# Fourth expert stage of a four-layer sequence model: down product in three rounded products, three chunks behind the gate

## The reference

```python
inh = sigmoid(x @ Wr / temperature)
w = routing weights from inh (zone, or the two nearest experts)
y = sum_e w[..., e] * ((silu(x @ Wg[e]) * (x @ Wu[e])) @ Wd[e])
out = x_residual + y
```

## Time and profile before

| | us |
|---|---|
| median of three runs | 1958.83 |
| lowest and highest | 1954.51, 1964.04 |
| the profiled execution | 1963.8 |
| its span, first to last instruction | 1961.8 |
| TensorE busy | 1723.9 |
| DVE busy | 1198.0 |
| ACT busy | 974.3 |
| POOL busy | 847.5 |

### The profile page before, as it was taken

The page is one execution under the profiler, slowest core; times in us unless marked ns, Lnnn a source line. Parts: engine busy times, 40 slices in busy tenths (PEclk is TensorE's granted clock), DMA queues, the critical chain, the costliest instruction groups (busy, mean ns, idle before and its releaser), DMA issues.

```text
span 1961.8 us, 25458 instructions
## 1 busy us (share of the span) xinstructions
PE 1723.9 (88%) x8004; PEld 1314.2 (67%) x8004; DVE 1198.0 (61%) x2815; ACT 974.3 (50%) x1864; POOL 847.5 (43%) x852
## 2 busy tenths in 40 slices
PE   6989998659999998989999988888899888888799
PEld 6979997537767676767777655666665555555565
DVE  5552215658677767777776835544446666677765
ACT  3612002346556665665656567676545444445442
POOL 3842101225545454554555454443447666651100
PEclk9989558769999999999999989898999888889999
DMA  5001000168433333233324462231000101112233
GB/s 84 1 2 24 1 1 1 38 146 201 111 92 102 87 98 92 90 99 86 96 90 118 114 161 73 58 88 47 17 23 23 33 23 26 23 28 75 81 106 94
DMA packets 131182, 134.92 MB, mean 69 GB/s; under 512 B 56614, under 2 KB 75306, under 8 KB 131050
## 3 DMA queue, kind: packets, MB, share of 16 engines
q1 hardware_dynamic: 120904, 132.35, 25.3%
q10 hardware_dynamic: 10146, 0.94, 0.6%
HBM read 127.93 MB, written 5.31 MB: 68 GB/s over the span
## 4 chain that ended last, share of the span: by engine, by line
PE 36%; DVE 17%; ACT 11%; issue 7%; POOL 4%; DMA 2%; SPq 1%; DVEq 0%; ACTq 0%; POOLq 0%
PE ypsum L1122 7%; PE flow_G L100 4%; PE flow_G L102 3%; PE flow_G L101 3%; DVE flow_a L1666 2%; DVE flow_a L1672 2%; DVE flow_phi L1450 2%; DMA flow_raw<-in_L_ffn_expert_down_k 2%; POOL flow_alo L1753 2%; PE flow_U L100 2%; PE flow_U L101 2%; PE flow_U L102 1%; ACT flow_ahi L1152 1%; ACT xn_tokens L1184 1%; PE flow_side L100 1%
## 5 line engine op out<-in xcount | busy, mean ns | idle before, releaser
L1753 POOL TENSOR_TENSOR flow_alo<-flow_a,flow_ahi 128x512 fp32r<-128x512 f32 x264 | 342.0, 1295 | 345.6 <-ACT flow_ahi L1152 345.1
L100 PE MATMUL flow_G<-xn_hi,flow_hi 128*128 128x512 f32 x520 | 285.6, 549 | 49.5 <-DVE flow_a L1666 23.2
L1666 DVE TENSOR_TENSOR flow_a<-flow_G,flow_mask 128x512 f32<-128x512 f32 x256 | 175.7, 686 | 161.2 <-ACT flow_G L1326 137.9
L1326 ACT ACTIVATE flow_G<-flow_G 128x512 f32<-128x512 f32 x256 | 149.0, 582 | 140.2 <-PE flow_G L102 139.7
L101 PE MATMUL flow_G<-xn_lo,flow_hi 128*128 128x512 f32 x520 | 213.0, 410 | 0.0
L102 PE MATMUL flow_G<-xn_hi,flow_lo 128*128 128x512 f32 x520 | 211.7, 407 | 0.0
L1672 DVE TENSOR_TENSOR flow_a<-flow_U,flow_a 128x512 f32<-128x512 f32 x296 | 204.7, 691 | 9.9
L1152 ACT ACTIVATE flow_ahi<-flow_a 128x512 fp32r<-128x512 f32 x264 | 165.4, 627 | 85.3 <-DVE flow_a L1672 84.1
L1762 POOL TENSOR_TENSOR flow_b<-flow_b,flow_mask 128x512 f32<-128x512 f32 x96 | 127.1, 1329 | 147.3 <-ACT flow_b L1330 76.7
L100 PEld LDWEIGHTS flow_G<-xn_hi,flow_hi 128*128 128x128 f32 x520 | 102.7, 197 | 117.6 <-issue 44.6
L1762 POOL TENSOR_TENSOR flow_a<-flow_a,flow_mask 128x512 f32<-128x512 f32 x96 | 127.8, 1343 | 106.3 <-ACT flow_a L1330 54.7
(11 more groups left out here) (536 smaller groups left out, 3930.1 us busy)
## 6 DMA issues: line engine op xcount, KB each, us to landing
flow_mask<-mask_rows_top SPq DMA_DIRECT2D x512, 128.0 KB, 3.1
flow_mask<-mask_rows_top SPq DMA_DIRECT2D x64, 256.0 KB, 3.3
flow_mask<-mask_rows_zone SPq DMA_DIRECT2D x64, 256.0 KB, 3.2
flow_mask<-mask_rows_steps SPq DMA_DIRECT2D x32, 256.0 KB, 4.0
x<-in_L_attn_x SPq DMA_DIRECT2D x8, 256.0 KB, 5.5
flow_raw<-in_L_ffn_expert_gate_k SPq DMA_DIRECT2D x16, 128.0 KB, 3.6
flow_raw<-in_L_ffn_expert_up_k SPq DMA_DIRECT2D x16, 128.0 KB, 3.6
flow_raw<-in_L_ffn_expert_down_k SPq DMA_DIRECT2D x16, 128.0 KB, 4.1
```

The lines of the kernel that those rows point to most:

```text
L100: pe.matmul(out, w_hi, x_hi, start=start, stop=False)
L1326: act.activation(gate, gate, ACT.Silu).then_inc(ev["r_done"], 1)
L1666: dve.tensor_tensor(out, G[at % 2].psum[:, :], weight, ALU.mult).then_inc(ev["t_done"], 1)
L1753: pool.tensor_tensor(alo[i][:, :], acts[i][:, :], ahi[i][:, :].bitcast(F32), ALU.subtract)\
```

## The change

The fourth stage goes over to the first stage's way. Its down matrix is split too (three matrices in place of two), ACT rounds each chunk's activations, POOL makes the low part, TensorE does three rounded products in place of one f32 product, and it does them three chunks behind the gate in place of five. SiLU writes one of the four activation tiles; it waits for the down product four chunks back. The copy waits for the stage's own count of DVE products. The step "y" of the fourth stage comes two chunks earlier (0.9 in place of 3), and that of the other three stages 0.1 earlier (2.9 in place of 3), which puts it one iteration of ACT's loop earlier, ahead of that iteration's SiLU.

```diff
+        self.split = index in (0, 3)
...
-MOE_STEPS = joined(post_steps(3), {"act": ((3, "y"),), "sp": ((5.5, "store"),)})
+MOE_STEPS = [joined(post_steps(3), {"act": ((0.9 if l == 3 else 2.9, "y"),), "sp": ((5.5, "store"),)}) for l in range(4)]
...
+        def parts_no(at):
+            return at if at < first else at - hosts[3].first + first
+
         def wait_slot(eng, at):
 
+            if plan.chunk[at][0].split and at >= hosts[3].first + A_RING:
+                eng.wait_ge(ev["down_done"], at - A_RING + 1)
+                return
             eng.wait_ge(ev["down_done"], at - B_RING + 1 if at >= first + B_RING else first - A_RING + at % A_RING + 1)
 
         def b_tile(at):
+            if plan.chunk[at][0].split:
+                return acts[at % A_RING]
             return B[(at - first) % B_RING]
...
-                    if h.direct:
+                    if h.split:
+                        pe.wait_ge(ev["ahi_done"], parts_no(at) + 1)
+                        pe.wait_ge(ev["alo_done"], parts_no(at) + 1)
+                    else:
                         wait_filled(pe, at)
-                    else:
-                        pe.wait_ge(ev["ahi_done"], at + 1)
-                        pe.wait_ge(ev["alo_done"], at + 1)
...
-                    if h.direct:
+                    if not h.split:
...
-                downs = [(at + (DIRECT_LAG if h.direct else DOWN_LAG), at) for at, (h, _, _) in enumerate(plan.chunk)]
+                downs = [(at + (DOWN_LAG if h.split else DIRECT_LAG), at) for at, (h, _, _) in enumerate(plan.chunk)]
...
-                    n = len(moe.sources) - 1
+                    n = len(moe.sources) - (not hosts[h].split)
...
-                    act.wait_ge(ev["a_done"], at + 1)
+                    act.wait_ge(ev["a_done"], plan.up[at])
...
-                    if at and at - 1 < first:
+                    if 0 < at <= plan.end and plan.chunk[at - 1][0].split:
                         rounded(at - 1)
...
-                    pool.wait_ge(ev["ahi_done"], at + 1)
+                    pool.wait_ge(ev["ahi_done"], parts_no(at) + 1)
...
-                    if at and at - 1 < first:
+                    if 0 < at <= plan.end and plan.chunk[at - 1][0].split:
                         rest(at - 1)
```

More of the change, by code:

```diff
@@ L655, in steps @@
             for g in range(GROUPS):
-                out += [(self.place("moe", l, g, off), name, "moe", l, g) for off, name in MOE_STEPS[engine]
+                out += [(self.place("moe", l, g, off), name, "moe", l, g) for off, name in MOE_STEPS[l][engine]
                         if l < 3 or name in LAST_STEPS]
```

## The result

The changed kernel takes 1979.88 us (median of four runs, 1972.88 to 1982.99), the kernel before 1959.19 us in the four runs beside it: ratio 1.010, 95% interval 1.0069 to 1.0131. It is about 20 us slower, outside the range and on the side of rival (b). The profiled execution took 1982.99 us with a span of 1981.0 us and a granted clock of 0.911 (before 1963.8, 1961.8 and 0.916).

A forecast was written before the change was run, and what follows sets the result against it. TensorE was taken as the bound in three fourth-stage stretches, with DVE or ACT leading elsewhere. Terms -5.6 - 0.9 - 1.6 + 5.6 + 1.5 = -1.0 us gave a median of 1957.8 us, range 1947 to 1968.

The forecast's parts named there:

- rival (b): Fourth stage's 27 DVE-bound chunks: every mask product meets POOL's low part, 13 us lost, 1969.3 us; chance 0.12.
- ACT's copies: Fourth stage, where ACT loads tables: copies waiting for DVE delay the affinities queued behind; 5.6 us lost, bounds 1.9 and 8.
- the meeting: DVE-bound stretches of the fourth stage: POOL's low part overlaps DVE once in each of three, 1.5 us lost, bounds 0 and 13.
- the form's gain: Fourth stage's TensorE-bound stretches: three rounded products in place of one f32 save 0.15 us on 37 chunks, 5.6 us gained.
- The price of a chunk: TensorE-bound stretches of the fourth stage: a chunk takes 2.10 us in place of 2.25, saving 0.15.
- the tail's term: End of the fourth stage: lag three in place of five, y about 3.5 us after the last up multiplication starts, 0.9 gained.
- decision point: DVE-bound chunks: POOL makes DVE the bound once more than half of those mask products are over 1 us.
- those 27 chunks: Fourth stage's chunks in 1764:1803, 1827:1859 and 1889:1903, where DVE is the bound; 0.48 to 0.5 us lost each.
- the stage's start: Chunk 4 of the fourth stage: two more down products, 1.4 us of TensorE, costed within the copies' term.
- The order of y: y ahead of one SiLU delays it at group ends: taken as nothing, bounds 0 and 0.3 for each of 32 groups, 10.
- the sum's -1.6: First stage: the first down product's wait for y, 1.6 us in all, goes and is gained.
- Splits: Fourth stage's eight splits, done in the second stage, grow from two to three matrices: nothing, at most 2 us.

The follow-up runs named there:

- with y at 1: Changed kernel with the fourth stage's y at 1 in place of 0.9, one ACT iteration later: 1977.3 us, ratio 1.0060 to 1.0112, stage 214.7 us.
- the mask product from PSUM: Changed kernel with the fourth stage's SiLU left in its bank, so DVE's mask product reads PSUM and one SBUF tile: 1976.9 us, stage 212.2 us.
- the copy's other 3 us: Changed kernel with POOL copying the activations in place of subtracting: 1971.4 us; stage 6.0 us longer than with the fill, 2.8 seen in DVE's durations.
- a fill: Changed kernel with POOL filling the low part's tile with zeros in place of subtracting: 1966.4 us, ratio 1.0021 to 1.0057, stage 204.2 us.

## Why the prediction was wrong, point by point

The account of the stage: 197.3 before; -1.0 for the form itself without its helpers; +7.9 for ACT's copies; +11.0 for POOL's low part; 215.1. Split at the last gate product, the part ahead of it has +1.8, +7.5 and +9.6, the end -2.8, +0.4 and +1.4. Beside the forecast, two terms carry most of the miss of 22 us: the meeting (1.5 forecast, 9.6) and the form's gain (-5.6 forecast, +1.8).

- **The price of a chunk: right.** 2.10 to 2.11 us wherever TensorE led, and taking one more product away gave 8.0 us where the count of 37 chunks said 8.5. The method, distances between starts in a stretch that TensorE leads, holds.
- **The meeting of POOL and DVE: the step that failed.** "I take one meeting of 0.5 in each of three stretches, 1.5 us"; the low part cost 9.6 us ahead of the last gate product (and 1.4 at the end, which the tail's term had), near the upper bound of 13 and rival (b). Two errors. The argument that POOL's start "hangs on DVE's own product" fixes where the low part begins, not what DVE does then: right behind the product come scans, pair products and the next mask product. And "an overlap costs DVE some 0.5 us" was read from one meeting in which DVE started halfway through POOL's instruction; where it started 0.10 us after POOL, ending 0.55 behind it all the same, it lost 1.09. Here one mask product cost 0.88 more, two scans 1.42, and a pair product at 1916.91 took 1.40 in place of 0.42. The Trainium skill's rule, with up to a whole low part of 1.29 us a meeting, was the better price. What no run settles is how 13 us of DVE's time became 9.6: with y at 1, DVE is 4.4 us shorter for 0.4 us, and with the mask product from PSUM 7.0 shorter for 3.0. Rival (b) had its place and its loser right and its size nearly. Its decision point, more than half of the mask products of those 27 chunks over 1 us, was wrong: only 15 of all 64 did it, since the scans and pair products carry their share, and they hang on the chain that sets the next gate product.
- **ACT's copies: mechanism right, size off.** 5.6 us forecast with bounds 1.9 and 8, measured 7.9 in the stage without POOL's part. The affinities came late as told, but not everywhere: TensorE's wait for them is 6.4 us in all against 2.5, 4.6 of it in the second stretch, 1.5 in the last routing and 0.3 in the first stretch, where it waits for y instead. What the sum missed is the stage's start, which was "costed within" this term. The first copy waits for a down product of the third stage ahead of ACT's exponentials, and y, which TensorE now needs two chunks sooner, comes behind a copy:

```profile
1765.98 0.63 ACT L1161 ACTIVATE flow_ahi<-flow_a 128x512 fp32r<-128x512 f32 x1 [1.01 <-PE ypsum L1131]
...
1766.63 1.28 ACT L1304 ACT_TABLE_LOAD   x1
```

  Counted from the stage's first gate product, this table load is 1.6 us later than before and y 2.2, and chunk 4 to 5 is where the largest single loss sits.
- **The form itself: the second step that failed, +1.8 in place of -5.6** ahead of the last gate product (the -1.0 of the account holds 2.8 gained behind it, where this kernel has neither copy nor low part to wait for). Without the helpers the kernel loses 3.7 us up to chunk 5, where the two more down products, and TensorE's waits for DVE, y and the affinities, fall; I had 1.4 and hid it. Another 2.3 go at chunks 27 to 29 and 1.0 at 43 to 44, where the clock is lower than before. Between these places TensorE gains its 0.15 a chunk.
- **The tail.** 3.9 us from the last up multiplication to y (3.6 forecast, 4.5 before): 0.6 gained, not 0.9, as TensorE waits for the low part twice.
- **The order of y: 0 was nearly right for the fourth stage, by luck, and wrong elsewhere.** It is worth half a microsecond in the new form. In the form that I reasoned from, it costs 5.2 us in two traces, within the bounds of 0 and 10. In the second stage, where I took nothing, it costs some 3 us. In the first stage the wait of 1.6 us went, and none of it was time: the sum's -1.6 was nothing.
- **Splits.** Nothing of it shows: with y at 2.9 the second stage takes 239.9 and 240.8 us in the two kernels with the old splits, and 239.3 in the median of the 14 with the wider ones.
- **The clock.** I gave it no term. It is one: in the form without helpers it took back the gains of two places (2.3 and 1.6 us), part of the 7.4 missed there. Of the changed kernel's 18 us it is a small part as far as tried: 10.2 us less of the lower clock gave 0.7.

The medians differ by 20.7 us, the fourth stage by 17.9; the second stage's 3.0 (237.1 to 240.1) is about the rest. What stays open: the copy's other 3 us, the clock's part at chunks 4 and 5, and why the median with the fourth stage's y earlier rose by 0.9 us only.

## What to carry to other kernels

Before giving an idle POOL a product beside a busy DVE, count DVE's instructions with two SBUF inputs in the window in which POOL will read, all of them and not only the one that triggers it, and price each meeting at what is then left of POOL's instruction, up to the whole. Count them where DVE leads; elsewhere they cost nothing here. A copy that waits for another engine costs little where it runs and much by what is queued behind it: list ACT's side steps behind each new wait. When two forms differ in how far their consumers lag, the change from one to the other is a place of its own in the sum, with its work, its waits and the clock after them.

## What the runs showed of the hardware that I had not expected

- A POOL instruction that only writes SBUF left 62 of DVE's two-input products at 659 to 694 ns, all but the first two of a stage; one that reads stretched them to as much as 1780 ns. Every mask product so stretched ended 0.55 to 0.56 us after POOL's instruction, whenever it had started.
- DVE instructions of less than two SBUF tiles can meet POOL too. A TENSOR_SCALAR on 128x32 elements took 1.09 us in place of 0.17 beside a low part (at 1790.56), and 0.29 beside a fill, ending 0.04 us after it:

```profile
1780.64 0.53 POOL L1763 MEMSET flow_alo<- 128x512 f32 x1 [1.57 <-ACT flow_ahi L1161]
...
1780.92 0.29 DVE L1546 TENSOR_SCALAR flow_zone_parts<-flow_affinity 128x32 f32<-128x32 f32 x1
```

- POOL pays as well: its low part, 1.29 us in the first stage, took 1.37 us on average in the fourth:

```profile
L1762 POOL TENSOR_TENSOR flow_alo<-flow_a,flow_ahi 128x512 fp32r<-128x512 f32 x64 | 87.5, 1368 | 106.6 <-ACT flow_ahi L1161 106.5
```

- The length of the fourth stage, 197.26 and 197.22, 202.48 and 202.47 us in pairs of executions with the same stage, repeats to 0.05 us, while whole executions of one kernel differ by some 10 us. A part of the trace can settle what the medians can't.
- The lower clock costs little where it meets a wait: between starts of products it is 0.43 in place of 0.24 us, yet 10.2 us less of it gave the changed kernel 0.7 us. Where it lay on the path, at chunks 43 to 45, it cost 2.3.
